# L1 attention on one core: all probabilities of seven heads and L1's v turned by VectorE and moved through DRAM, late q units between the first four scores

## The reference, cut to what matters

```python
q = (query @ Wq + bq).reshape(B, L, NKV, G, HDIM)
k_, v_ = jnp.split(kv @ Wkv + bkv, 2, axis=-1)
scores = jnp.einsum('blkgd,bmkd->bkglm', q, k) * scale
attn = jax.nn.softmax(scores, axis=-1)
o = jnp.einsum('bkglm,bmkd->blkgd', attn, v).reshape(B, L, NHEAD * HDIM)
return o @ Wo + bo
```

## Time and profile before

| | us |
|---|---|
| median of 3 runs | 1112.55 (1112.52 to 1113.59) |
| the profiled execution, its time | 1113.17 |
| its span, first to last instruction | 1111.1 |
| PE busy | 1092.7 (98%) |
| DVE, ACT, POOL busy | 554.7, 514.4, 411.8 |
| one head of the L1 loop | 71.3 |
| mean granted clock of PE | 0.998 of 2.4 GHz |

### The profile page before, as it was taken

How to read it: one execution, slowest core, us unless ns; L and a number is a source line. 1 busy time by engine, 2 the same in 40 slices (tenths; PEclk the granted TensorE clock), 3 DMA queues, 4 the chain that set the end, 5 groups by cost and what they waited for, 6 DMA issues and landing times.

```text
span 1111.1 us, 14739 instructions
## 1 busy us (share of the span) xinstructions
PE 1092.7 (98%) x5258; PEld 884.8 (80%) x5258; DVE 554.7 (50%) x1018; ACT 514.4 (46%) x1430; POOL 411.8 (37%) x277
## 2 busy tenths in 40 slices
PE   8999999999999999999999999999999999999997
PEld 5888888887877688877888888888888888888875
DVE  5464366357477533484534535345254353443654
ACT  5475376357475322456615436254262351633521
POOL 3252044024266653577403306024051240512672
PEclk9999999999999999999999999999999999999999
DMA  8111001010000221102131121220211202111002
GB/s 249 29 47 30 1 29 30 1 48 10 1 19 1 104 95 39 38 1 77 40 112 40 38 76 38 63 88 33 81 38 52 99 16 98 38 45 53 1 18 76
DMA packets 41997, 55.21 MB, mean 50 GB/s; under 512 B 20484, under 2 KB 32004, under 8 KB 39268
## 3 DMA queue, kind: packets, MB, share of 16 engines
q1 hardware_dynamic: 41956, 54.67, 15.1%
HBM read 44.69 MB, written 5.77 MB: 45 GB/s over the span
## 4 chain that ended last, share of the span: by engine, by line
PE 89%; DVE 4%; ACT 3%; POOL 1%; issue 1%; DMA 1%; SPq 0%; POOLq 0%; DVEq 0%; ACTq 0%
PE work L637 14%; PE work L639 14%; PE work L638 14%; PE work L696 8%; PE yb L637 5%; PE yb L639 5%; PE yb L638 5%; PE pt L709 4%; PE ov L637 3%; PE ov L639 3%; PE ov L638 3%; PE pt L639 3%; PE pt L638 3%; PE pt L637 3%; ACT prob L1188 1%
## 5 line engine op out<-in xcount | busy, mean ns | idle before, releaser
L1412 POOL TENSOR_TENSOR prob<-prob,exp_rcp 128x512 f32<-128x512 f32 (+1 forms) x96 | 127.4, 1327 | 506.0 <-DVE exp_rcp L1675 506.0
L1188 ACT ACTIVATE prob<-work,neg_max 128x128 f32<-128x128 f32 (+1 forms) x384 | 149.4, 408 | 63.5 <-DVE neg_max L1700 63.5
L637 PE MATMUL work<-xT_hi,q_hi 128*128 128x512 f32 x416 | 168.1, 404 | 0.4 <-DVE xT_lo L1782 0.4
L638 PE MATMUL work<-xT_lo,q_hi 128*128 128x512 f32 x416 | 164.4, 395 | 0.0
L639 PE MATMUL work<-xT_hi,q_lo 128*128 128x512 f32 x416 | 164.4, 395 | 0.0
L696 PE MATMUL work<-kT,qT 128*128 128x128 f32 (+1 forms) x704 | 112.9, 303 | 0.1
L696 PEld LDWEIGHTS work<-kT,qT 128*128 128x128 f32 (+1 forms) x704 | 102.8, 191 | 11.8 <-issue 0.3
L1144 ACT ACTIVATE oT_hi<-ov 32x128 fp32r<-32x128 f32 (+2 forms) x160 | 60.4, 377 | 106.3 <-PE ov L639 104.0
L1746 DVE TENSOR_TENSOR oT_lo<-ov,oT_hi 32x128 fp32r<-32x128 f32 (+2 forms) x160 | 67.4, 421 | 71.5 <-ACT oT_hi L1144 70.2
L1700 DVE TENSOR_REDUCE neg_max<-work 128x4 f32<-128x512 f32 (+1 forms) x96 | 82.9, 864 | 40.1 <-PE work L696 38.3
L637 PE MATMUL yb<-o_hi,oT_hi 128*128 128x512 f32 x224 | 93.3, 416 | 3.0 <-DVE oT_lo L1746 2.9
(11 more groups left out here) (226 smaller groups left out, 2136.2 us busy)
## 6 DMA issues: line engine op xcount, KB each, us to landing
raw<-in_l_q SPq DMA_DIRECT2D x8, 1024.0 KB, 5.4
raw<-in_l_o SPq DMA_DIRECT2D x8, 1024.0 KB, 4.8
kv_raw<-in_l_kv SPq DMA_DIRECT2D x8, 515.0 KB, 3.4
prob<-vT SPq DMA_DIRECT2D x128, 32.0 KB, 1.8
p_bounce<-bo_bc SPq DMA_DIRECT2D x14, 256.0 KB, 2.1
prob<-p_bounce SPq DMA_DIRECT2D x56, 64.0 KB, 2.0
raw<-in_l_o SPq DMA_DIRECT2D x4, 768.0 KB, 4.2
raw<-in_l_q SPq DMA_DIRECT2D x16, 144.0 KB, 2.7
```

The source lines that it names most:

```text
L637: pe.matmul(dst, l_hi, r_hi, start=first and k == 0, stop=False)
L638: pe.matmul(dst, l_hi, r_lo, start=False, stop=False)
L1188: e = act.activation(prob[:, i % 2, g * L.keys:(g + 1) * L.keys], s[:, g, :], ACT.Exp, bias=neg_max[:, i % 2, g:g + 1], accum_out=exp_sum[ ...
L1412: pool.tensor_tensor(p, p, exp_rcp[:, b % 2, :].unsqueeze(2).broadcast_to([P, G, L.keys]), ALU.mult)\
```

## The change

In the seven heads of the loop PE transposes no probabilities any more. All eight blocks go by DVE `turn_p`, a DRAM write, four DRAM reads and an SBUF-to-SBUF split (`back_upper` on ACT, `back_lower` on DVE). The DRAM buffer and the SBUF landing place alternate between two; SP's `move_p` is called for one block at a time and waits for the low part two blocks back before it reads into the same place. v goes through DRAM as well: one DMA out, four back, in place of 16. The units q 4 to 7 stand one each behind scores 0 to 3 (in the last head too: q6 behind scores 2, q7 behind scores 3). Values come three blocks behind scores, output four. Units of the next head are dealt 3, 2, 2, 1 to four closing steps. POOL's o_lo, kv_lo and q_lo each move one normalisation later in the loop's heads, ACT's o_hi behind the second exponentials and `next_weights` to steps 4, 5 and 6. SP's load of the next o moves behind the eight detours. Some semaphores that nothing uses are no longer made. The core of the diff:

```diff
-        self.q_steps = [(3, 4), (), (5,)] if sources == 2 else [(4,), (5,), (6, 7)]
+        self.q_steps = [(3, 4), (), (5,)] if sources == 2 else [(4,), (5,), (6,), (7,)]
...
+        TURN_AHEAD = (L1.ahead_all[0:3], L1.ahead_all[3:5], L1.ahead_all[5:7], L1.ahead_all[7:8])
...
+            def move_p(it, b):
+                sp.wait_ge(p_turned, it * NB + (b + 1))
+                sp.dma_start(bounce[b % 2], bo_bc[:, :]).then_inc(p_out, 16)
+                sp.wait_ge(p_out, it * (NB * 16) + 16 * (b + 1))
+                if b >= 2:
+                    sp.wait_ge(S1.pt_lo_done, it * NB + (b - 1))
+                blocks = bounce[b % 2].rearrange("(i t) (j c) -> j t i c", t=third, j=4)
+                for j in range(4):
+                    dst = prob[third * j:third * (j + 1), b % 2, HID:2 * HID].rearrange("t (i c) -> t i c", i=4)
+                    sp.dma_start(dst, blocks[j]).then_inc(p_back[b % 2], 16)
...
+                sp.dma_start(v_bounce, vT[:, TOK:2 * TOK]).then_inc(v_out, 16)
+                sp.wait_ge(v_out, it * 16 + 16)
+                parts = v_bounce.rearrange("(x t) (g c) -> g t x c", t=third, g=4)
+                for g in range(4):
+                    dst = vT[third * g:third * (g + 1), 0:TOK].rearrange("t (x c) -> t x c", x=4)
+                    sp.dma_start(dst, parts[g]).then_inc(v_back, 16)
...
                 load(kv_raw[:, 0:1030], A["l1_kv"][it], kv_loaded, kv_lo_done, it + L1.kv0)
                 load(q_raw[:, :], A["l1_q"][it], q_loaded, q_lo_done, it + L1.q0)
+                for b in range(NB):
+                    move_p(it - 1, b)
                 load(o_raw[:, :], A["l1_o"][it], o_loaded, o_lo_done, it + L1.o0)
-                move_p(it - 1)
                 move_v(it)
...
                         transpose_p(L, S, it, 0)
+                        if L.double:
+                            scores(L, S, it, 2)
                         project(L, S, it, "q", L.q_steps[2][0])
                         values(L, S, it, 0)
...
                             scores(L, S, it, i, norm)
+                            if i == 3:
+                                project(L, S, it, "q", L.q_steps[3][0])
                             values(L, S, it, i - 2)
```

The new head on PE:

```diff
+            def turned_head(L, S, it):
+                for i in range(NB + 4):
+                    if i >= NB:
+                        for kind, u in TURN_AHEAD[i - NB]:
+                            project(L, S, it + 1, kind, u)
+                    if i > 4:
+                        output(L, S, it, i - 4, (0, 1))
+                    if i < NB:
+                        scores(L, S, it, i)
+                    if i == 0:
+                        pe.wait_ge(N[2].lo, NB)
+                    if i < 4:
+                        project(L, S, it, "q", 4 + i)
+                    if i == 3:
+                        values(L, S, it, 0)
+                    if i == 4:
+                        output(L, S, it, 0, (0, 1))
+                    if NB <= i:
+                        output(L, S, it, i - 4, (2, 3))
+                    if 4 <= i < NB + 3:
+                        values(L, S, it, i - 3)
+                    if 4 <= i < NB:
+                        output(L, S, it, i - 4, (2, 3))
```

On ACT:

```diff
+            def back_upper(S, it, b):
+                act.wait_ge(p_back[b % 2], it * (NB * 32) + 64 * (b // 2 + 1))
+                act.activation(p_of(pT_hi[:, 0, :]), p_back_of(b), ACT.Copy).then_inc(S.pt_hi_done, 1)
...
+            def turned_head(L, S, it, next_kv, next_q):
+                for i in range(NB + 4):
+                    if i >= NB:
+                        evacuate(L, S, it + 1, *TURN_AHEAD[i - NB])
+                    if 3 <= i < NB + 3:
+                        back_upper(S, it, i - 3)
+                    if i < 5:
+                        exponentials(L, S, it, i)
+                    if 3 <= i < NB + 3:
+                        oT_upper(L, S, it, i - 3)
+                    if 5 <= i < NB:
+                        exponentials(L, S, it, i)
+                    if i == 0:
+                        evacuate(L, S, it, ("q", 4))
+                        upper_v(S, it)
+                    if i == 1:
+                        split_hi(o_hi, o_raw, 0, L.tiles * HID, P, o_loaded, S.scores_done, it + L.o0, it * NB + 1)\
+                            .then_inc(o_hi_done, 1)
+                    if i == 2:
+                        evacuate(L, S, it, ("q", 6))
+                    if i == 4:
+                        act.wait_ge(S.act_evac, L.evacuated(it, "q", 6))
+                    if i in (4, 5, 6):
+                        next_weights(L, S, it, i - 1, None, next_kv, next_q)
```

On POOL (kv_lo and the halves of q_lo take `late` in the same way):

```diff
+                late = 1 if L.double and norm is None else 0
                 for b in range(NB):
...
                     normalise(L, S, it, b)
-                    if b == 0:
+                    if b == late:
                         split_lo(o_of(L)[1], o_raw, o_of(L)[0], L.tiles * HID, P, o_hi_done, o_lo_done, it + L.o0)
```

On DVE (`reciprocals` waits for the exponentials and writes exp_rcp as before):

```diff
+            def back_lower(S, it, b):
+                dve.wait_ge(S.pt_hi_done, it * NB + (b + 1))
+                dve.tensor_tensor(p_of(pT_lo[:, 0, :]), p_back_of(b), p_of(pT_hi[:, 0, :]).bitcast(F32), ALU.subtract)\
+                    .then_inc(S.pt_lo_done, 1)
...
+            def turned_head(L, S, it):
+                negative_max(L, S, it, 0, False)
+                reciprocals(0)
+                turn_p(S, it, 0)
+                negative_max(L, S, it, 1, False)
+                lower_v(S, it)
+                reciprocals(1)
+                evacuate(L, S, it, ("q", 5))
+                negative_max(L, S, it, 2, False)
+                turn_p(S, it, 1)
+                reciprocals(2)
+                negative_max(L, S, it, 3, False)
+                back_lower(S, it, 0)
+                reciprocals(3)
+                turn_p(S, it, 2)
+                evacuate(L, S, it, ("q", 7))
+                oT_lower(L, S, it, 0)
+                back_lower(S, it, 1)
+                negative_max(L, S, it, 4, False)
+                turn_p(S, it, 3)
+                reciprocals(4)
+                oT_lower(L, S, it, 1)
+                for i in range(5, NB):
+                    add_share(L, S, it, i - 5, None)
+                    back_lower(S, it, i - 3)
+                    turn_p(S, it, i - 1)
+                    negative_max(L, S, it, i, False)
+                    oT_lower(L, S, it, i - 3)
+                    reciprocals(i)
+                for i in range(NB, NB + 4):
+                    add_share(L, S, it, i - 5, None)
+                    if i == NB:
+                        turn_p(S, it, NB - 1)
+                    evacuate(L, S, it + 1, *TURN_AHEAD[i - NB])
+                    if i < NB + 3:
+                        back_lower(S, it, i - 3)
+                        oT_lower(L, S, it, i - 3)
+                add_share(L, S, it, NB - 1, None)
```

More of the change, by code:

```diff
@@ L69, in __init__ @@
         for b in range(NB):
-            if b == 2:
+            if b == 2 and self.packed:
                 own += [("q", u) for u in self.q_steps[2]]
@@ L762, in attention_head @@
                         transpose_p(L, S, it, 0)
+                        if L.double:
+                            scores(L, S, it, 2)
                         project(L, S, it, "q", L.q_steps[2][0])
                         values(L, S, it, 0)
[L765 to L767 removed]
+                        if not L.double:
+                            scores(L, S, it, 2)
                     elif i < NB:
                         if L.double:
[L770 removed]
+                            transpose_p(L, S, it, i - 2)
                             output(L, S, it, i - 3, (0, 1))
                             scores(L, S, it, i, norm)
+                            if i == 3:
+                                project(L, S, it, "q", L.q_steps[3][0])
                             values(L, S, it, i - 2)
@@ L1214, in head, with exponentials @@
                         oT_upper(L, S, it, b)
+            def back_upper(S, it, b):
+                act.wait_ge(p_back[b % 2], it * (NB * 32) + 64 * (b // 2 + 1))
+                act.activation(p_of(pT_hi[:, 0, :]), p_back_of(b), ACT.Copy).then_inc(S.pt_hi_done, 1)
+            def exponentials(L, S, it, i):
+                act.wait_ge(S.max_done, it * NB + (i + 1))
+                bank = L.score_bank(i, False)
+                for g in range(G):
+                    e = act.activation(prob[:, i % 2, g * P:(g + 1) * P], work[:, bank, g * P:(g + 1) * P], ACT.Exp,
+                                       bias=neg_max[:, i % 2, g:g + 1], accum_out=exp_sum[:, i % 2, g:g + 1])
+                e.then_inc(S.exp_done, 1)
+            def turned_head(L, S, it, next_kv, next_q):
[22 more added lines that the diff above has]
+                        next_weights(L, S, it, i - 1, None, next_kv, next_q)
             def split_packed(it):
@@ L1648, in head @@
                         norm_lo(norm, 1)
-                    if L.double and norm is None and i == NB:
```

(8 more changed lines are left out.)

88 lines of the change are left out of this document (32 added, 56 removed).

## The result

The changed kernel takes 1162.32 us (median of 4, 1159.73 to 1163.94), the kernel before 1112.74 (median of 4): a ratio of 1.044, interval 1.042 to 1.047. The forecast was 1162, in a range of 1118 to 1174. The profiled execution took 1163.54 with a span of 1161.7, 50.6 more than before.

The account below looks back on a forecast made before the run. PE alone bounds the loop's heads. Stalls of 8.89 us less 2.64 removed make a head 6.25 longer, plus 0.7 for clock; seven heads plus 1.0 for the last give 49.7 on 1112.55: 1162 us, range 1118 to 1174.

Parts of the forecast that it names:

- scores(4): In each loop head, these scores wait for q7's evacuation and start at 17.04 instead of 15.46: 1.58 us.
- three outputs: In steps 5, 6 and 7 of a loop head, each output starts 0.22 us late behind its values: 0.67 us.
- Ceiling: Transposes taken from PE: 2.64 us a head, 18.5 us in seven heads, a head of 68.63 us at best.
- Lock rule: A DVE subtraction of two SBUF tensors (back_lower) that meets a POOL operation ends 0.55 us after it.
- The race of 0.18: POOL reaches q_lo 0.18 us before back_lower(3) is asked for; values 3 and 4 stall 2.60 and 2.61 us.
- rival (a): POOL doesn't win the races against back_lower(3) and (4): stalls 0.69 us each, 1131 us; chance 0.15.
- The detour: A block's way through DRAM, 5.4 us, stays hidden with 0.2 to 1 us of cover; blocks 3 and 4 have 3.
- The clock: PE's first 2.6 us gap loses clock in each head, mostly given back: 0.7 us a head stays.
- The last head: Behind the loop, transposes of block 1 wait for their normalisation behind o_lo: 1.0 us, bounds 0 to 1.6.
- Rival (b): The lock doesn't show, POOL's long pieces let DVE in: stalls of 3.4 us a head, 1119 us; chance 0.12.
- Rival (d): Both gaps of 2.6 us lose the clock in full, or DMAs land late under load: 1180 us; chance 0.06.
- Rival (c): Faster: the cover holds, scores(4) don't wait, stalls under 2.64 us a head; 1095 us with none; chance 0.07.

Follow-up runs that it names:

- e8: Changed kernel with POOL, ACT, DVE and PE queues reordered so long POOL pieces stay clear of back_lower, q7 moved in the last head: 1100.07 us, ratio 0.988.
- e1: Changed kernel with POOL's weight pieces behind normalisations 4, 5 and 6 waiting for back_lower 2, 3 and 4: 1123.2 us, ratio 1.009.
- e3: Changed kernel with eight unused matmuls ahead of the values of blocks 3 and 4, filling PE's gaps: 1159.09 us, ratio 1.041.
- e5: On top of e2, DVE evacuates q7 ahead of turn_p(2) instead of behind it: 1114.43 us, ratio 1.002.
- e9: Changed kernel with one extra DMA per block, from the DRAM buffer to spare DRAM, ahead of the four reads: ratio 1.047.
- e2: Changed kernel with ACT's next_weights behind back_upper instead of ahead of it: 1118.68 us, ratio 1.005.
- e7: Changed kernel with four extra DMAs per block, from the DRAM buffer to spare DRAM, ahead of the four reads: 1187.86 us, ratio 1.068.
- e6: Changed kernel with each of POOL's two halves of q_lo cut to half its columns, order unchanged: 1144.44 us in one run.

## Why the prediction was right

Point by point, t as in the prediction, measured in the head from 592.49:

| step | predicted | measured |
|---|---|---|
| POOL's o_lo | 9.42 to 14.04 | 9.39 to 13.99 |
| back_lower(0) ends | 14.59 | 14.54 |
| turn_p(2) ends, q7's evacuation ends | 16.27, 16.94 | 16.28, 16.91 |
| scores(4) start; stall | 17.04; 1.58 | 17.15; 1.71 |
| kv_lo | 22.06 to 24.45 | 22.28 to 24.66 |
| back_lower(2) starts, ends; stall | 22.50, 25.00; 1.16 | 22.75, 25.20; 1.20 |
| POOL ahead at q_lo | 0.18 | 0.20, 0.21 |
| stall at values(3), values(4) | 2.60, 2.61 | 2.56, 2.48 |
| three outputs | 0.67 | 0.21 + 0.27 + 0.27 = 0.75 |
| a head | 78.2 | 78.47 in the mean |
| last head | +1.0 | +1.3 |

- **Ceiling.** Right: e8 gets to within 0.7 us of it.
- **Lock rule.** Right, and the largest term: without three of its four meetings (e1) 39 of 50 us are gone, the clock's share with them. It was read from two places of the trace of before, none of them in the attention; its 0.55 came back at every meeting: in the traces of the changed kernel and of e1 to e3 and e5 to e9, 194 back_lower in the loop take longer than 0.72, and each ends 0.53 to 0.56 behind a POOL operation inside which it started. The Trainium skill's rule ("SBUF — State Buffer", section "SBUF: two separate sides") agrees in that whichever comes first keeps the other out, POOL too (e2). Read to the letter, the DVE operation would have ended 0.69 behind POOL's; the runs say 0.55.
- **The race of 0.18.** It went as forecast, at 0.20 or 0.21 in all seven heads; e2 shows that the other outcome would have been rival (a), at an even lower price.
- **scores(4).** The chain o_lo, normalisation 2, turn_p(2), evacuation is right to 0.1 us, and e5 confirms it. The 0.13 too little is the step from an evacuation's end to PE: 0.24, where I took 0.10.
- **The detour.** Hidden, as said; but the 3 us that the prediction left to blocks 3 and 4 can't be spent by all detours at once. e7 shows it: SP's cycle, 3.8 for one block and 6.8 in e7, is what has little room, and one late block pushes the next.
- **The clock.** The sum was right by luck, 0.7 forecast and 0.66 measured (the 4.6 us that e3 takes from seven heads); its form was not. I had every head lose the clock in the first gap and get most of it back. In fact each head has one stretch of seven or eight matmuls at the lower level (granted clock 0.50 from 634.30 to 636.70, that is 1.2 GHz), 0.43 apart instead of 0.23, some 1.5 us in all. It lies either ahead of values(4), where the wait for POOL swallows it (704.45 to 711.67, head of 77.79), or behind them, where nothing does (632.33 to 640.00, head of 79.29). Three of the seven heads are of the second kind; why they alternate is open.
- **The last head.** Half right. The wait for normalisation 1 behind o_lo is there, 0.95 where 1.0 was forecast. But the wait that ends last is another, which the prediction saw in the loop and not here: the output of block 0 for the split of its values, 1.32 in all, inside the bounds.

Rival (b), no lock, falls with e1 and e6. Rival (d), both gaps at the lower clock in full or late DMAs, falls with e3 and e9 (its own sum gives 1183 and not 1180). Rival (c) needs other queues than the change has: with those of e8 the cover holds, at 1100 where 1095 was the price without any stall. There ACT already waits 1.09 us for the reads of block 4, without holding PE. The Trainium skill ("VectorE: DVE Perf Modes", section "Rules for kernel authors") would leave a 128x128 transpose to TensorE; the changed kernel, 4.4% slower, agrees; e8 doesn't, in which DVE turns 56 blocks and the whole is 1.2% faster than the kernel before.

## What to carry to other kernels

Moving work off the engine that bounds a kernel is worth its price only if the new consumers find their operands in time: write out one period of every queue before building it. When an operand moves from PSUM to SBUF, ask what else its reader then meets: here a DVE subtraction of two SBUF tensors ended 0.55 us behind each POOL operation that it met, so it has to be kept clear of long ones, by order or by an explicit wait. And an engine that is idle for half the time can still be late; e1 added a wait on POOL and gained 39 us on the changed kernel.

## What the runs showed of the hardware that was not expected

- How much POOL is held: q_lo takes 2.60 us where it starts 0.34 before back_lower ends (e2), 2.34 to 2.40 where it doesn't meet one. The prediction had counted on the like for normalisation 2 without a row for it, and rightly: the two normalisations from 606.45 take 2.48 in the changed kernel, where two others take 2.08.
- A DMA issue of SP takes 0.44 us in a row of four that starts alone (1.73 to 1.76), 0.50 when the row stands right behind another DMA (2.01, e7 and e9) and 0.62 for the DMAs from DRAM to DRAM (2.46 for four, e7).
- The last stage of the kernel loses the clock by different amounts: the part behind the last scores had 0.96 and took 58.6 us in the kernel before, 0.98 and 58.5 us in the changed one. In the profiled execution of e3 (1161.96) it took 61.5 us, and the 20 us from 1140 had 0.79. So little of the 4.6 us that its heads gain is left in that execution's time:

```profile
1140.00:1160.00 20.00, 13.38 (x44) 8.43 (x42) 9.86 (x25) 3.93 (x7) 3.83 (x3) 0.79 0.28 105
```
